# Neighbour maximum on TensorE: the key products of a step stand between the ranks and the second pick

## The chip, the cores and the metric

The kernel runs on one core of a Trainium2 chip. The metric is device time in microseconds (us) of one launch, with every input in device memory; the figure given for a kernel is the median of its runs.
## The reference

```python
def reference(x, adj, W, a):             # x (4096,128) f32, adj (4096,4096) int32, 0 or 1
    # layer 0: maximum over the neighbours, feature by feature
    h = jnp.maximum(_layernorm(x), 0.0)
    masked = jnp.where((adj != 0)[:, :, None], h[None, :, :], neg)
    x = x + jnp.max(masked, axis=1)       # in chunks of rows; 0 where a row has no neighbour
    # layer 1: graph attention
    h = jnp.maximum(_layernorm(x), 0.0)
    h = h @ W
    e = (h @ a[:128])[:, None] + (h @ a[128:])[None, :]    # a is (256, 1), one column
    e = jnp.where(e > 0, e, 0.2 * e)
    attention = jax.nn.softmax(jnp.where(adj > 0, e, -9e15), axis=1)
    return x + elu(attention @ h)
```

A row of `adj` has some 17 neighbours among 4096 columns. The change lies in layer 0, the neighbour maximum.

## The kernel before

Layer 0 goes over `adj` in 8 tiles of 512 rows (`TILES`), and over the columns of a tile in 16 pairs of 128-column chunks (`STEPS`): 128 steps g (`PAIRS`). Chunks of 128 columns hold few neighbours of a row, mostly none, one or two. A step picks the first and the second of them exactly by matmuls and raises a running maximum with them; what is left over (a third neighbour, and one that a shared second pick can't take) is left to a search by keys and to gathers from a table in device memory.

TensorE does these parts for a step, all in the function `_(pe)` of the tensor block:

- turns (`flip`, L581 to L594): 8 transposes of `adj` from `stage` into `flip_ps`, for step g + 5. They wait for the load, and for ScalarE's copy of the turned block before (`edge_ready`).
- ranks (`rank`, L596 to L606): 2 matmuls of 512 columns into `order_ps`, for step g + 3; in some steps (`shared`) a third, the nudge (L605). They wait until ScalarE has read `order_ps` of the step before (`depth_ready`).
- first and second pick (`pick`, L608 to L627): 4 matmuls of 512 columns each, with the high and the low half of h as weights, into `pick_ps[0]` and `pick_ps[1]`. Each waits until VectorE has taken the maximum of the same buffer in the step before (`raised`).
- key products (`digest(n, half)`, L629 to L641): 8 matmuls of 128 columns into `key_ps`. A group n covers two steps' `rest` masks and is done in two halves: half 0 in the even step g = 2n + 2, half 1 in the odd step 2n + 3. Half 0 waits for the masks and for `keyed`, n: ScalarE must have copied the keys of group n - 1 out of `key_ps`. For odd n it begins with one matmul of 512 columns, the word (L635). `flip_ps` and `key_ps` are the two halves of `late_ps`, one bank each.

ScalarE does in step g, in this order: `edges(g + 4)` (L393, copy of the turned block, waits for `flipped`), in even steps `key(g // 2 - 2)` (L423, copy of the keys, waits for `digested`), `select(g + 3)` (L404 `first` and L405 `depth`, waits for `ordered`, the ranks), and in even steps `later` (L413, masks).

VectorE does in step g: `take(g, 0)` (L882, the maximum with the first pick), then in some steps `rests` (L870) or `seconds` (L864), `take(g, 1)` (with the second pick; half as wide where `shared`), and after that, in some steps, a subset table entry (L857, steps 0 to 10), `fold` (L886, once in 16 steps), the `search` of keys (L890, once in four steps) and `halve_two` (L898 to L904, three of eight steps).

SyncE loads `stage` (L277, 1 MB for two steps, four stages, waits for `flipped`) and stores the turned edges for layer 1 (L284). GpSimd issues the gathers (L376), paced by `raised`. Each engine runs its list strictly in the order in which it is written out; the semaphores order the engines among each other.

The order on TensorE is written by hand, in the loop at L739: first pick of g, ranks of g + 3, second pick of g, turns of g + 5, key products. Layer 1 (L762 on) begins with the last key products and then mixes, for 256 blocks, weights that VectorE makes (L1072).

Of the kernel before, what the change touches and what calls it, by code (L numbers as in the profile page):

```python
# [86 lines left out]
def layers(nc, adj, x_rows, w, a, edge_units, subset_max, out_rows, w_sb, a12, w_in, hs, x1_in, h_hi, h_lo, ident_h, ident32, order_w, bit_w, word,  # L87
# [4 lines left out]
    with ctx:  # L92
# [73 lines left out]
        def rest_done(eng, m):  # L166
            if m % 2 == 0:
                eng.wait_ge(rest_even, m // 2 + 1)
            else:
                eng.wait_ge(rest_odd, 2 * (m // 2 + 1))  # L170
# [4 lines left out]
        def shared(g):  # L175
            return g % 8 in (2, 4, 6) or g < len(CHAINS)
# [10 lines left out]
        spare = lambda i: keys[:, 1, i, :].rearrange("p (g d) -> p g d", d=D) if i < ROWS else left[:, (i - ROWS) * GROUPS:(i - ROWS + 1) * GROUPS, :]  # L187
        saves = lambda i: 16 * (len(range(i, len(CHAINS), SPARES)) + (2 if i == 3 else 0))
        slot_of = {m: i % SPARES for i, (m, _, _) in enumerate(CHAINS)}
        many_of = lambda m: one_of(SINGLES[m]) if m in SINGLES else spare(slot_of[m])  # L190

# [80 lines left out]
        with nc.Block() as block:  # L272
# [307 lines left out]
            def _(pe):  # L580
                def flip(g):  # L581
                    n, s = g // KEEP, g % KEEP
                    if s == 0:
                        pe.wait_ge(landed[n % STAGES], 16 * (n // STAGES + 1))
                    if g == 0:
                        pe.wait_ge(consts_made, 1)
                    if g >= 1:
                        pe.wait_ge(edge_ready, g)
                    for c in range(PAIR):
                        for r in range(ROWS):  # L590
                            low = stage[:, n % STAGES, r, :].bitcast(F16).rearrange("p (j t) -> p j t", t=2)[:, :, 0]
                            last = nc.tensor.transpose(flip_ps[:, c * TI + r * P:c * TI + (r + 1) * P],  # L592
                                                       low[:, (s * PAIR + c) * P:(s * PAIR + c + 1) * P], ident_h[:, :])
                    last.then_inc(flipped, 1)  # L594

                def rank(g):  # L596
                    pe.wait_ge(edge_ready, g + 1)
                    if g >= 1:
                        pe.wait_ge(depth_ready, g)
                    for c in range(PAIR):  # L600
                        nudged = c == 1 and shared(g)
                        last = nc.tensor.matmul(order_ps[:, c * TI:(c + 1) * TI], order_w[:, :], edge_t[:, g % (KEPT * KEEP), c * TI:(c + 1) * TI],  # L602
                                                start=True, stop=not nudged)
                        if nudged:
                            last = nc.tensor.matmul(order_ps[:, TI:W], nudge_w[:, :], edge_t[:, g % (KEPT * KEEP), 0:TI], start=False, stop=True)  # L605
                    last.then_inc(ordered, 1)  # L606

                def pick(g, k):  # L608
                    p = g % STEPS
                    if k == 0:  # L610
                        pe.wait_ge(first_ready, g + 1)
                        if g < STEPS // 4:
                            pe.wait_ge(lo_first, 1)
                        elif g < STEPS:
                            pe.wait_ge(lo_ready, g * PAIR // EIGHTH - 1)
                    else:
                        pe.wait_ge(second_ready, g // 2 + 1)
                    if g >= 1:
                        pe.wait_ge(raised, 2 * (g - 1) + k + 1)
                    s = first[:, g % 4, :] if k == 0 else second[:, g % 4, :]  # L620
                    together = k == 1 and shared(g)
                    for c in range(PAIR):
                        to = 0 if together else c * TI
                        for part, half_h in enumerate((h_hi, h_lo)):
                            last = nc.tensor.matmul(pick_ps[k][:, to:to + TI], half_h[:, p * PAIR + c, :], s[:, c * TI:(c + 1) * TI],  # L625
                                                    start=part == 0 and not (together and c), stop=part == 1 and (c == 1 or not together))
                    last.then_inc(picked, 1)  # L627

                def digest(n, half):  # L629
                    if half == 0:  # L630
                        rest_done(pe, n)
                        if n >= 1:
                            pe.wait_ge(keyed, n)
                        if n % 2:
                            nc.tensor.matmul(key_ps[:, :], ones_h[:, :], word[:, :].rearrange("p (r w) -> p r w", r=1).broadcast_to((P, ROWS, P)), start=True, stop=False)  # L635
                    for r in range(half * ROWS // 2, (half + 1) * ROWS // 2):
                        for b in range(QUAD):
                            g, c = 2 * n + b // PAIR, b % PAIR
                            last = nc.tensor.matmul(key_ps[:, r * P:(r + 1) * P], rest[:, g % RESTS, c * TI + r * P:c * TI + (r + 1) * P],  # L639
                                                    bit_w[:, b, :], start=n % 2 == 0 and r == 0 and b == 0, stop=r == ROWS - 1 and b == QUAD - 1)  # L640
                    last.then_inc(digested, 1)  # L641

                def rows(g):
                    if g == 0:
                        pe.wait_ge(depth_ready, PAIRS)
                        pe.wait_ge(folded, 2)
                    elif g == 2:
                        pe.wait_ge(folded, 4)
                        pe.wait_ge(raised, 2 * PAIRS - 1)
                    elif g == 4:  # L650
                        pe.wait_ge(col_took, 4)
                    elif g == 5:
                        pe.wait_ge(limited, 3)
                    elif g == 6:
                        pe.wait_ge(col_took, 5)
                    elif g == LAST:
                        pe.wait_ge(folded, TILES)
                        pe.wait_ge(joined, LAST)
                    for c in range(ROWS):
                        last = nc.tensor.transpose(row_ps(g)[:, c * P:(c + 1) * P], best[:, (g * ROWS + c) * P:(g * ROWS + c + 1) * P], ident32[:, :])  # L660
                    last.then_inc(rows_put, 1)

                def columns(g):
                    if g == 0:
                        pe.wait_ge(small_took, 3)
                    elif g == 1:
                        pe.wait_ge(col_took, 1)
                    elif g in (2, 3):
                        pe.wait_ge(wh_made, ROWS)
                    elif g in (4, 5):  # L670
                        pe.wait_ge(joined, 6)
                    else:
                        pe.wait_ge(col_took, g)
                    pe.wait_ge(h_made, (g + 1) * ROWS)
                    for c in range(ROWS):
                        last = nc.tensor.transpose(col_ps(g)[:, c * P:(c + 1) * P], h[:, g * ROWS + c, :], ident32[:, :])
                    last.then_inc(col_put, 1)
# [61 lines left out]
                for g in range(PAIRS):  # L739
                    if g:  # L740
                        pick(g, 0)
                    if g + 3 < PAIRS:
                        rank(g + 3)
                    if g == PAIRS - 4:
                        pe.wait_ge(edge_ready, PAIRS)
                        pe.wait_ge(w_in, 48)
                        nc.tensor.transpose(wt_ps, w_sb[:, 0:D], ident32[:, :]).then_inc(small_put, 1)
                    if g == PAIRS - 3:
                        pe.wait_ge(small_took, 1)
                        pe.wait_ge(wide_made, 2)  # L750
                        nc.tensor.matmul(wa_ps, w_t[:, :], a_wide[:, :], start=True, stop=True).then_inc(small_put, 1)
                        rows(0)
                        rows(1)
                    pick(g, 1)
                    if g + AHEAD < PAIRS:
                        flip(g + AHEAD)
                    if g >= 2:
                        digest(g // 2 - 1, g % 2)
                columns(0)
                rows(2)  # L760
                rows(3)
# [549 lines left out]
```

## Time and profile before

| What | Value |
|---|---|
| median of 3 runs | 725.0 us (722.88 to 726.06) |
| the profiled execution | 728.94 us |
| its span, first to last instruction | 727.0 us |
| mean granted clock of TensorE | 0.990 |
| layer 0's steps | about 38 to 457 us of the span |
| mean DMA bandwidth | 227 GB/s |

All rows are of the profiled execution. Timelines give the start of an instruction and its recorded length; successive instructions of an engine are pipelined, so that recorded lengths overlap. The distance between two starts is what an instruction costs its engine when it does not wait. An idle time is given in brackets, with the engine and line that ended it.

### The profile page before, as it was taken

The numbers are of one execution on the slowest core, as the hardware profiler recorded it, in microseconds if no ns is written. First come the engines' busy times: TensorE is split into PE (matmuls) and PEld (weight loads), VectorE is DVE, ScalarE is ACT, GpSimd is POOL, SyncE is SP. The second block draws the span as 40 slices with busy tenths as digits, with TensorE's granted clock in tenths as the row PEclk, the third lists the DMA queues.
The fourth block names the chain that finished last, engine by engine and source line by source line (L and its number), as shares of the span: only waits on it lengthen the run. The fifth ranks groups of instructions, "written<-read, shape, count | busy, mean of one in ns | idle before, by whom it ended". The sixth has DMA issues, their size and how long they took to land.

```text
span 727.0 us, 14879 instructions
## 1 busy us (share of the span) xinstructions
PE 678.4 (93%) x5615; PEld 498.6 (69%) x5615; DVE 662.0 (91%) x1038; ACT 474.6 (65%) x692; POOL 265.4 (37%) x263
## 2 busy tenths in 40 slices
PE   1799999999999999999999997799989999999994
PEld 1355565656656556556555554798979999999994
DVE  8999799999999999999999999989987988888883
ACT  2898899999999999999999994644232301101100
POOL 0532046556555554556656563544410000000000
PEclk9999999999999999999999999999999999999997
DMA  9999988998889888888888646343423553435300
GB/s 300 302 354 387 389 284 286 325 363 287 270 272 288 292 276 286 258 284 291 287 275 273 210 142 240 94 145 128 143 89 105 189 198 131 174 132 181 124 16 18
DMA packets 64026, 165.19 MB, mean 227 GB/s; under 512 B 6929, under 2 KB 11665, under 8 KB 59857
## 3 DMA queue, kind: packets, MB, share of 16 engines
q1 hardware_dynamic: 53776, 138.75, 54.6%
q0 software_dynamic: 10176, 25.44, 13.3%
q8 instruction: 48, 0.79, 0.4%
q14 instruction: 26, 0.20, 0.1%
HBM read 119.60 MB, written 44.56 MB: 226 GB/s over the span
## 4 chain that ended last, share of the span: by engine, by line
PE 72%; DVE 13%; DMA 7%; issue 4%; ACT 3%; POOL 1%; DVEq 0%; SPq 0%; ACTq 0%; POOLq 0%
PE pick_ps L625 25%; PE pick_ps L726 21%; PE late_ps L592 6%; PE late_ps L639 6%; PE order_ps L602 6%; DVE acc L882 4%; PE late_ps L726 4%; DMA found<-subset_max,tops 4%; DMA edge_units<-edge_t 3%; DVE rest L1072 2%; PE order_ps L605 1%; POOL found L376 1%; ACT depth L405 1%; PE late_ps L635 1%; DVE acc L1001 1%
## 5 line engine op out<-in xcount | busy, mean ns | idle before, releaser
L376 POOL DMA_INDIRECT found<-subset_max,tops x224 | 238.0, 1062 | 222.0 <-DVE tops L890 102.9
L882 DVE TENSOR_TENSOR acc<-pick_ps,acc 128x1024 f32<-128x1024 f32 (+1 forms) x248 | 272.7, 1100 | 18.9 <-PE pick_ps L625 12.7
L726 PE MATMUL pick_ps<-keys,rest 128*128 128x129 f32 x1792 | 208.9, 277 | 7.2 <-DVE rest L1072 7.2
L726 PEld LDWEIGHTS pick_ps<-keys,rest 128*128 128x128 f32 x1792 | 204.9, 193 | 12.0 <-DVE rest L1072 9.5
L1072 DVE SCALAR_TENSOR_TENSOR rest<-depth,curves_sb,stage 128x512 f32<-128x512 f32 x256 | 183.1, 747 | 20.7 <-PE pick_ps L726 5.0
L404 ACT ACTIVATE first<-order_ps 128x1024 f16<-128x1024 f32 x128 | 131.3, 1025 | 16.3 <-PE order_ps L605 8.4
L405 ACT ACTIVATE depth<-order_ps 128x1024 f16<-128x1024 f32 x128 | 130.6, 1020 | 0.0
L592 PEld LDWEIGHTS late_ps<-ident_h,stage 128*128 128x128 f16 x1024 | 68.9, 100 | 49.9 <-DMA stage<-adj 13.1
L625 PE MATMUL pick_ps<-first,h_hi 128*128 128x512 f16 x256 | 97.5, 381 | 3.3 <-DVE acc L882 3.2
L625 PE MATMUL pick_ps<-second,h_hi 128*128 128x512 f16 x256 | 97.4, 381 | 3.1 <-DVE acc L882 3.0
L625 PE MATMUL pick_ps<-first,h_lo 128*128 128x512 f16 x256 | 97.5, 381 | 0.0
L625 PE MATMUL pick_ps<-second,h_lo 128*128 128x512 f16 x256 | 97.5, 381 | 0.0
L592 PE MATMUL late_ps<-ident_h,stage 128*128 128x128 f16 x1024 | 80.1, 222 | 17.4 <-DMA stage<-adj 13.1
L393 ACT ACTIVATE edge_t<-late_ps 128x512 int32<-128x512 int32 x128 | 77.1, 602 | 7.1 <-DMA edge_units<-edge_t 4.3
L602 PE MATMUL order_ps<-edge_t,order_w 128*128 128x512 f16 x256 | 77.5, 385 | 3.6 <-ACT depth L405 3.6
L639 PE MATMUL late_ps<-bit_w,rest 128*128 128x128 f16 x1024 | 78.3, 220 | 0.0
L518 ACT ACTIVATE keys<-pick_ps,acc 128x128 f32<-128x128 f32 x28 | 8.0, 368 | 100.0 <-DVE acc L1083 99.2
L639 PEld LDWEIGHTS late_ps<-bit_w,rest 128*128 128x128 f16 x1024 | 64.4, 98 | 5.4 <-issue 0.6
L413 ACT ACTIVATE rest<-depth 128x1024 f16<-128x1024 f16 x64 | 67.8, 1060 | 0.0
L381 POOL DMA_DIRECT2D out<-keys x7 | 5.4, 770 | 158.4 <-DVE keys L1105 158.4
L625 PEld LDWEIGHTS pick_ps<-second,h_hi 128*128 128x128 f16 x256 | 25.0, 98 | 38.7 <-issue 10.6
L602 PEld LDWEIGHTS order_ps<-edge_t,order_w 128*128 128x128 f16 x256 | 24.5, 98 | 35.3 <-issue 8.1
(152 smaller groups left out, 600.1 us busy)
## 6 DMA issues: line engine op xcount, KB each, us to landing
stage<-adj SPq DMA_DIRECT2D x64, 1024.0 KB, 7.1
edge_units<-edge_t SPq DMA_DIRECT2D x64, 512.0 KB
stage<-edge_units SPq DMA_DIRECT2D x32, 1024.0 KB, 4.8
subset_max<-keys POOLq DMA_DIRECT2D x9, 512.0 KB, 10.9
found<-subset_max,tops POOLq DMA_INDIRECT x224
best<-x SPq DMA_DIRECT2D x4, 512.0 KB, 6.1
subset_max<-x POOLq DMA_DIRECT2D x4, 512.0 KB, 7.6
subset_max<-left POOLq DMA_DIRECT2D x4, 512.0 KB, 9.8
```

Source lines behind the costliest of these rows:

```text
L376: nc.gpsimd.indirect_dma_start(found[:, n % NG, s, :], None, subset_max, bass.IndirectOffsetOnAxis(tops[:, n, s:s + 1], 0)).then_inc(gathe ...
L393: nc.scalar.activation(edge_t[:, g % (KEPT * KEEP), :].bitcast(I32), flip_i[:, :], ACT.Copy, scale=ONE_BITS).then_inc(edge_ready, 1)
L404: nc.scalar.activation(first[:, g % 4, :], order_ps[:, :], ACT.Sigmoid, scale=-SHARP, bias=SHARP * (0.5 - MARK)).then_inc(first_ready, 1)
L405: nc.scalar.activation(depth[:, g % 4, :], order_ps[:, :], ACT.Abs, bias=MARK - MID).then_inc(depth_ready, 1)
L413: nc.scalar.activation(rest[:, to, :], depth[:, g % 4, :], ACT.Sigmoid, scale=-STEEPER, bias=STEEPER * LATE).then_inc(rest_odd, 1)
L592: last = nc.tensor.transpose(flip_ps[:, c * TI + r * P:c * TI + (r + 1) * P], low[:, (s * PAIR + c) * P:(s * PAIR + c + 1) * P], ident_h[: ...
L602: last = nc.tensor.matmul(order_ps[:, c * TI:(c + 1) * TI], order_w[:, :], edge_t[:, g % (KEPT * KEEP), c * TI:(c + 1) * TI], start=True, ...
L625: last = nc.tensor.matmul(pick_ps[k][:, to:to + TI], half_h[:, p * PAIR + c, :], s[:, c * TI:(c + 1) * TI], start=part == 0 and not (toget ...
L639: last = nc.tensor.matmul(key_ps[:, r * P:(r + 1) * P], rest[:, g % RESTS, c * TI + r * P:c * TI + (r + 1) * P], bit_w[:, b, :], start=n % ...
L726: last = nc.tensor.matmul(out_ps(q, b), weight[:, n % WEIGHTS, b * P:(b + 1) * P], wh[:, c, :], start=c == 0 and starts(q, b), stop=c == C ...
L882: V.tensor_tensor(acc[:, q % 2, 0:cols], pick_ps[k][:, 0:cols], acc[:, q % 2, 0:cols], ALU.max).then_inc(raised, 1)
L1072: V.scalar_tensor_tensor(out=weight[:, n % WEIGHTS, :], in0=limit[:, q % 4, :], scalar=slope[:, c:c + 1], in1=units[:, m % EDGES, k * TI:( ...
```

## The change

The call of `digest` moves from the end of the step's body to the place between the ranks (and what is inserted in two of the last steps) and the second pick. Which key products a step does, all waits inside `digest`, `pick` and `flip`, and all other engines' lists stay as they were.

```diff
@@ -751,11 +751,11 @@
                         nc.tensor.matmul(wa_ps, w_t[:, :], a_wide[:, :], start=True, stop=True).then_inc(small_put, 1)
                         rows(0)
                         rows(1)
+                    if g >= 2:
+                        digest(g // 2 - 1, g % 2)
                     pick(g, 1)
                     if g + AHEAD < PAIRS:
                         flip(g + AHEAD)
-                    if g >= 2:
-                        digest(g // 2 - 1, g % 2)
                 columns(0)
                 rows(2)
                 rows(3)
```

## Rows read from the trace of the kernel before

**Rows 1.** The page, busy us by engine (share of the span) and instructions.
```profile
PE 678.4 (93%) x5615; PEld 498.6 (69%) x5615; DVE 662.0 (91%) x1038; ACT 474.6 (65%) x692; POOL 265.4 (37%) x263
```

**Rows 2.** Windows: stretch, length, busy us of PE, PEld, DVE, ACT, POOL; clock, DMA share, GB/s.
```profile
260.00:340.00 80.00, 79.43 (x665) 47.70 (x662) 77.16 (x86) 77.02 (x101) 43.16 (x43) 1.00 0.87 277
```

**Rows 3.** Timeline of TensorE, an odd step's end and an even step: start, us, engine, operation.
```profile
301.29 0.38 PE L625 MATMUL pick_ps<-second,h_hi 128*128 128x512 f16 x1
...
302.60 0.61 PE L639 MATMUL late_ps<-bit_w,rest 128*128 128x128 f16 x8
303.05 0.38 PE L625 MATMUL pick_ps<-first,h_hi 128*128 128x512 f16 x1
...
303.91 0.59 PE L602 MATMUL order_ps<-edge_t,order_w 128*128 128x512 f16 x2
304.34 0.38 PE L625 MATMUL pick_ps<-second,h_hi 128*128 128x512 f16 x1
...
305.65 0.38 PE L635 MATMUL late_ps<-word,ones_h 128*128 128x512 f16 x1
```

**Rows 4.** The chain that ended last, by time: first and last of twelve like pieces.
```profile
131.69 0.88 PE pick_ps L625 x4
...
415.95 0.88 PE pick_ps L625 x4
```

**Rows 5.** Timeline of TensorE, the step of the cycle in which it waits for VectorE.
```profile
316.55 0.59 PE L602 MATMUL order_ps<-edge_t,order_w 128*128 128x512 f16 x2
317.33 0.38 PE L625 MATMUL pick_ps<-second,h_hi 128*128 128x512 f16 x1 [0.19 <-DVE acc L882]
```

**Rows 6.** Timeline of VectorE ahead of that wait.
```profile
305.85 0.68 DVE L882 TENSOR_TENSOR acc<-pick_ps,acc 128x512 f32<-128x512 f32 x1
306.45 0.94 DVE L898 TENSOR_TENSOR found<-found 128x768 f32<-128x768 f32 x1
307.38 1.22 DVE L882 TENSOR_TENSOR acc<-pick_ps,acc 128x1024 f32<-128x1024 f32 x1
...
312.78 1.22 DVE L890 MAX8 tops<-keys 128x8 int32<-128x1024 f32 x1
313.92 0.41 DVE L904 TENSOR_TENSOR left<-found 128x256 f32<-128x256 f32 x1
314.24 1.22 DVE L882 TENSOR_TENSOR acc<-pick_ps,acc 128x1024 f32<-128x1024 f32 x1
...
315.97 1.22 DVE L882 TENSOR_TENSOR acc<-pick_ps,acc 128x1024 f32<-128x1024 f32 x1
```

**Rows 7.** Timeline of ScalarE beside the steps of rows 3 and rows 5.
```profile
301.49 1.02 ACT L404 ACTIVATE first<-order_ps 128x1024 f16<-128x1024 f32 x1
...
303.32 0.60 ACT L393 ACTIVATE edge_t<-late_ps 128x512 int32<-128x512 int32 x1
303.80 0.62 ACT L423 ACTIVATE keys<-late_ps 128x512 f32<-128x512 f32 x1
...
306.37 1.06 ACT L413 ACTIVATE rest<-depth 128x1024 f16<-128x1024 f16 x1
...
316.43 0.62 ACT L423 ACTIVATE keys<-late_ps 128x512 f32<-128x512 f32 x1
```

**Rows 8.** Timelines of ScalarE and TensorE near 79 us, behind a DMA.
```profile
78.34 0.60 ACT L393 ACTIVATE edge_t<-late_ps 128x512 int32<-128x512 int32 x1 [2.04 <-DMA edge_units<-edge_t]
78.84 0.59 ACT L423 ACTIVATE keys<-late_ps 128x512 f32<-128x512 f32 x1
...
79.00 0.62 PE L592 MATMUL late_ps<-ident_h,stage 128*128 128x128 f16 x8 [1.10 <-ACT edge_t L393]
...
79.57 0.61 PE L639 MATMUL late_ps<-bit_w,rest 128*128 128x128 f16 x8
...
81.41 0.59 PE L602 MATMUL order_ps<-edge_t,order_w 128*128 128x512 f16 x2 [0.36 <-ACT depth L405]
```

**Rows 9.** Timeline of VectorE at the end of layer 0, step 125.
```profile
438.99 1.23 DVE L882 TENSOR_TENSOR acc<-pick_ps,acc 128x1024 f32<-128x1024 f32 x1 [0.81 <-PE pick_ps L625]
```

## The prediction

> **What bounds the kernel now.** I read the page's busy shares first [rows 1]: TensorE is busy 93% of the span and VectorE 91%, so the page alone names no bound. The table of windows for the middle of layer 0 [rows 2] shows three engines close together: of 80 us TensorE is busy 79.4, VectorE 77.2, ScalarE 77.0, at a clock of 1.00, the full level of 2.4 GHz. Two things can thus set a step's time: TensorE's own work, or a loop of waits through two engines. So I went to the timelines and took the distance from one start to the next as an operation's price (recorded durations overlap).
>
> TensorE, in step g [rows 3]: first pick 0.86 (303.05 to 303.91), ranks 0.43 (303.91 to 304.34), second pick and turns 1.31 (301.29 to 302.60), of which the second pick, as large as the first, is 0.86 and the turns 0.45, key products 0.45 (302.60 to 303.05). Together 3.05 us. A single 512-column matmul is a quarter of 0.86, 0.215: the nudge adds one in three of eight steps, the word matmul one in two of eight. A cycle of eight steps is 24.4 + 1.1 = 25.5 us of pure issue. The chain that ended last repeats the same pieces every 25.84 us, twelve times [rows 4], where the first and the last of the twelve stand, 284.26 us apart. The missing 0.35 us is one visible wait per cycle: ranks start at 316.55 and could be followed at 316.98, but the second pick starts at 317.33, released by VectorE [rows 5]. It waits for the maximum of the previous step's second pick, which VectorE starts only at 315.97, because a search (1.14) and a halving (0.32) stood ahead of it in VectorE's order [rows 6]. So layer 0 is bound by TensorE's issue, plus 0.35 us in one step of eight.
>
> **The change, part by part.** Nothing is added or removed; the eight (or nine) key products of a step move ahead of second pick and turns, 1.31 us earlier in the step.
>
> (a) The wait on VectorE goes. In the step of 316.55 the key products, with their word, take 0.67 us, so the second pick is asked at 317.65 at the earliest, after 317.33. Gain 0.35 x 12 = 4.2 us. What is late next there? I laid VectorE's operations on the new order, (b) included, by [rows 6]: a maximum 1.13 and `seconds` or `rests` 0.60 (together 1.73, 314.24 to 315.97; the search, as wide as a maximum, is 1.14), a shared maximum 0.60, halvings 0.93, 0.60 (as wide as the shared maximum) and 0.32. Count from the start of a step g with g % 8 = 4: it and the next start at 0, 3.48, 6.53, 9.79 and 13.06, and a maximum starts 0.23 after its pick. VectorE ends its first maximum at 2.23, the shared one at 3.86, the halving at 4.79; in the next step maximum 5.93, `seconds` 6.53, maximum 7.67, halving 8.27; in the third maximum 9.41, shared maximum (from 9.57) 10.17, search 11.31, halving 11.63; in the fourth the maximum 12.77. The first pick at 13.06 needs that one, 0.15 us to spare with the 0.14 that (b) finds for a way between engines. Everywhere else there is more. So VectorE binds nowhere, by a small margin. The fold of every 16th step, 0.6 us, falls where VectorE has over 1 us of room.
>
> (b) A new wait comes, on ScalarE. The first half of the key products, in even steps, overwrites the PSUM region that ScalarE's key copy (L423) reads, and waits for `keyed`. ScalarE does, in an even step: edge copy, key copy, the two outputs of select, perhaps later. In the step of 303.05 the key copy starts at 303.80 and lasts 0.62, so it ends at 304.42 [rows 7]. Now the products are asked at 305.65, and it is long done. In the new order they are asked when the ranks end, at 304.34 [rows 3]: 0.08 us before the copy has ended. To that comes the way from ScalarE to TensorE. Two places near 79 us show it [rows 8]: the edge copy ends at 78.94 and the turns start at 79.00 (0.06); the key copy ends at 79.43 and key products that waited for it start at 79.57 (0.14). The second is the same pair of operations, so I take 0.14. The wait is 0.08 + 0.14 = 0.22 us. The step of the VectorE wait gives the same: copy 316.43 + 0.62 + 0.14 = 317.19 against 316.98, 0.21 [rows 5, 7]. The Trainium skill, page Perfetto Trace Analysis, section Per-instruction lifecycle, says that a semaphore reaches other engines after the recorded end of a ScalarE instruction; with that delay at nothing the wait would be 0.08 us a time and 4.3 us in all; the trace agrees with the page.
>
> Does this wait recur, or does ScalarE catch up once? I followed the loop from the odd step's ranks. They end at 301.29; first starts at 301.49 (0.20 later), select takes 1.83 to 303.32, the edge copy 0.48, the key copy 0.62, the way 0.14: 3.27 us from ranks to the moment the next even products may start [rows 3, 7]. TensorE's own path between the same two points is, in the new order, products, second pick, turns, first pick, ranks: 0.45 + 0.86 + 0.45 + 0.86 + 0.43 = 3.05. Both start at the same event, so the 0.22 returns in every pair of steps; in the old order the path had 1.31 more and hid it. The loop then goes on behind the wait through second pick, turns, first pick and ranks, and TensorE does not get the time back. ScalarE's own work of a pair (two selects of 1.83, two edge copies, key copy, `later` of 1.06 at most, each from [rows 7]) is at most 6.3 us, in truth less, as recorded durations overlap, against 6.3 or more for the pair, so it gives nothing back either. Could the edge copy be late, since its turns now end the previous step? They end 1.76 us after the ranks, plus 0.20 for the way 1.96, while ScalarE is free at 2.03: covered, by 0.07.
>
> The even steps 16 to 122 are 54. At 0.215 each: 11.6 us.
>
> (c) Steps before 16. Here stores of edges hold ScalarE up (2.04 us idle for a DMA) [rows 8], so a small wait ahead of such a place costs nothing. But at the last of them, near 78 us, second pick and turns used to come before the key products or right at the edge copy; now the products wait until 79.57 and both follow (0.86 + 0.45). The odd step's ranks had waited for ScalarE until 81.41, and ended at 82.05; in the new order they end at 79.57 + 0.45 + 1.31 + 0.86 + 0.65 = 82.84. Cost 0.8 us. For the two earlier places I take nothing, since the next store sets the time again. Bounds: 0 and 3 x 0.8 = 2.4.
>
> (d) The end of the stage. At step 124 the wait falls where TensorE next waits for ScalarE anyway. In step 125 the products stand before a second pick for which VectorE is idle 0.81 us [rows 9], and VectorE then runs the layer's end: +0.45. In steps 126 and 127 VectorE is far behind TensorE: nothing. Bounds 0 and 0.9 (twice 0.45).
>
> (e) Queues. Turns end 0.67 us or so later in a step, and with them the loads of `stage` that SyncE issues; a load has four stages, seven steps, ahead of its use. The stores wait for edge copies, which move with the step. GpSimd's gathers are paced by `raised`, which shifts by as little. Nothing. Layer 1 has the same order and moves as a block.
>
> Sum: 11.6 - 4.2 + 0.8 + 0.45 = 8.65 us. Against the profiled execution, span 727.0 gives 735.6 and its own 728.94 gives 737.6. The median of three runs, 725.0, lies 3.9 under that execution; on it I predict 733.6 us, 1.2% slower.
>
> **The rivals.**
> *The key copy is in time* (chance 0.12). If ScalarE's copy ran ahead by 0.22 us, from edges ready earlier or ranks that no longer start late, only (a) is left, with (c) and (d): -4.2 + 1.25 = -3.0, 722.0 us. It ends not slower. The place is the wait on `keyed` in even steps, its price 0.215 x 54; it decides at a copy that ends 0.22 earlier. For it: the miss is small beside a copy of 0.62. Against: both paths start at the same ranks [rows 3, 7], in all four even steps of the cycle.
> *The VectorE wait stays too* (0.15). If the 0.15 us of margin in (a) isn't there, TensorE waits for ScalarE in each even step and once per cycle for VectorE. At most the 4.2 of (a) come back: 737.8 us. For it: VectorE at 77.2 of 80 [rows 2]. Against: the longer cycle, about 26.3, gives VectorE 0.5 us more room.
> *The wait is longer than its two terms* (0.08). If the turns, now last in a step, make the edge copy late, say by 0.1 more than the 0.07 of cover, all 54 pairs get 0.1 longer: 5.4 us, 739.0 us.
> *The clock falls* (0.03). In the stretches with waits of 0.35 us the granted clock was 1.00 [rows 2, 5], the 2.4 GHz level. If the many short waits lowered it to 1.2 GHz in a tenth of layer 0's 350 us, issue there would take twice as long, 35 us: 769 us. The Trainium skill, page TensorE: Matmul & The Clock Gate, section A second HAM failure mode, tells of a kernel whose frequent micro-idles made the clock swing; by that rule this rival would be likely; the trace speaks against it as far as it goes.
>
> **How the numbers follow.** Forecast 0.62, the rivals 0.12, 0.15, 0.08 and 0.03. The forecast's own range: the wait between 0.14 (way 0.06) and 0.28 gives -4.1 and +3.5; (c) and (d) give -1.25 and +2.05: 728.3 to 739.2. The range of 8 in 10 takes in the third and part of the second case down to 727 and up to 740. A measurement tells 0.5%, about 3.6 us, from no change. Slower by more: the forecast nearly whole and three rivals, 0.83; within: most of the first rival and the low edge of the forecast, 0.13; faster by more: 0.04, a copy in time with (c) and (d) at nothing, 720.8.
>
> **What would show it.** In the timeline after: key products following the ranks with an idle of 0.2 us in even steps, released by ScalarE L423, and no idle before the products of odd steps; second picks without the wait on VectorE; a cycle of about 26.3 us in place of 25.84. (b) is wrong if the even products follow the ranks without idle; (a) if second picks still wait for VectorE; (c) if ranks near 82 us don't shift. I would be wrong altogether if the cycle fell under 25.84.

## The result, and the profile after

| | before | after |
|---|---|---|
| median of 5 runs | 725.36 us (722.88 to 726.06) | 732.34 us (731.36 to 733.41) |
| the profiled execution | 728.94 us | 733.41 us |
| its span | 727.0 us | 731.6 us |

The ratio of after to before is 1.0094, with a 95% interval of 1.0064 to 1.0125: slower by 7.0 us. The forecast was 733.6 us and slower. A second job gave the changed kernel (4 runs) 732.06 us beside 725.72 us, ratio 1.0099 (1.0063 to 1.0135). All ratios leave out the few executions over 1.5% above the fastest of their kernel, which the medians keep (at most one of a kernel, but two of twelve in the second job with the key copy first).

The page of after, busy shares; it answers to [rows 1] and says as little:

```profile
PE 683.4 (93%) x5615; PEld 495.4 (68%) x5615; DVE 664.0 (91%) x1038; ACT 478.8 (65%) x692; POOL 269.2 (37%) x263
```

The windows of after (stretch, length, busy us of PE, PEld, DVE, ACT, POOL, then clock, DMA share, GB/s), beside [rows 2]: TensorE looks exactly as busy, VectorE and ScalarE each a little less. The clock is 1.00 here, and over 84 to 440 us as well, so the rival of the falling clock is out.

```profile
260.00:340.00 80.00, 79.42 (x645) 45.95 (x643) 76.20 (x84) 76.46 (x99) 43.72 (x43) 1.00 0.90 277
```

TensorE's timeline of after, an odd step and the start of the next even one (start, us, engine, operation), to be held against [rows 3]:

```profile
303.55 0.59 PE L602 MATMUL order_ps<-edge_t,order_w 128*128 128x512 f16 x2
303.98 0.38 PE L605 MATMUL order_ps<-edge_t,nudge_w 128*128 128x512 f16 x1
304.20 0.61 PE L639 MATMUL late_ps<-bit_w,rest 128*128 128x128 f16 x8
304.65 0.38 PE L625 MATMUL pick_ps<-second,h_hi 128*128 128x512 f16 x1
...
305.51 0.61 PE L592 MATMUL late_ps<-ident_h,stage 128*128 128x128 f16 x8
305.96 0.38 PE L625 MATMUL pick_ps<-first,h_hi 128*128 128x512 f16 x1
...
306.82 0.59 PE L602 MATMUL order_ps<-edge_t,order_w 128*128 128x512 f16 x2
307.46 0.38 PE L635 MATMUL late_ps<-word,ones_h 128*128 128x512 f16 x1
```

In the odd step nothing waits: 303.98 + 0.215 = 304.20, the key products' start. In the even step the ranks take 0.43, to 307.25, and the products (their word) start at 307.46: a wait of 0.21 us. ScalarE's timeline names the cause, as [rows 7] foretold it:

```profile
304.40 1.02 ACT L404 ACTIVATE first<-order_ps 128x1024 f16<-128x1024 f32 x1
305.32 1.02 ACT L405 ACTIVATE depth<-order_ps 128x1024 f16<-128x1024 f32 x1
306.22 0.60 ACT L393 ACTIVATE edge_t<-late_ps 128x512 int32<-128x512 int32 x1
306.70 0.62 ACT L423 ACTIVATE keys<-late_ps 128x512 f32<-128x512 f32 x1
```

The odd ranks end at 304.20, `first` starts 0.20 later, the key copy ends at 307.32, and 0.14 later the products start. From ranks to products it is 3.26 us (predicted 3.27), against 3.05 of TensorE's own work. Two words that stand eight steps apart give the cycle:

```profile
307.46 0.38 PE L635 MATMUL late_ps<-word,ones_h 128*128 128x512 f16 x1
...
333.79 0.38 PE L635 MATMUL late_ps<-word,ones_h 128*128 128x512 f16 x1
```

26.33 us, where [rows 4] had 25.84. The wait on VectorE of [rows 5] is gone. The summary of waits (who waited, for whom: us in total, times, longest us) of before has it, 180 to 340 us:

```profile
PE pick_ps L625 <- DVE acc L882: 1.1, 6, 0.2
```

After has no such row between 180 and 420 us. Nor has it a row of matmuls for the new wait. It lists for TensorE only weight loads, put down to "issue", 180 to 340 us:

```profile
PEld late_ps L635 <- issue: 6.2, 12, 0.5
PEld late_ps L639 <- issue: 6.2, 12, 0.5
```

These two rows do point at the place. Before has none for L635 and L639 in this stretch, and their 24 times are one for each of its even steps. But they name no releaser, and 0.5 us is not what the wait costs.

The recorded length of the ranks, 0.59, covers most of a wait of 0.21 that begins 0.43 after their start. Only 0.05 is left as idle time, some twelve times in 80 us. That comes to the 0.58 us that TensorE is idle now, as the three recorded waits of 0.19 on VectorE made the 0.57 before: two different losses leave the same busy share. 54 waits of 0.21 are 11 us, and what each costs only the distance between starts shows.

### The profile page after: what moved, and what is told of

Read it like the earlier page. It is cut to its first block, busy times and chain, and to the rows that moved or that the text cites. A ratio compares the mean times of both kernels' runs of the same rounds, so it can differ in the third digit from the quotient of the medians.

```text
span 731.6 us, 14879 instructions
## 1 busy us (share of the span) xinstructions
PE 683.4 (93%) x5615; PEld 495.4 (68%) x5615; DVE 664.0 (91%) x1038; ACT 478.8 (65%) x692; POOL 269.2 (37%) x263
## 4 chain that ended last, share of the span: by engine, by line
PE 78%; DVE 8%; DMA 7%; ACT 3%; issue 2%; POOL 1%; SPq 0%; DVEq 0%; ACTq 0%; POOLq 0%
PE pick_ps L625 27%; PE pick_ps L726 21%; PE late_ps L639 8%; PE late_ps L592 7%; PE order_ps L602 7%; PE late_ps L726 4%; DMA found<-subset_max,tops 4%; DMA edge_units<-edge_t 2%; DVE rest L1072 2%; PE order_ps L605 1%; PE late_ps L635 1%; POOL found L376 1%; ACT depth L405 1%; DVE acc L1001 1%; DMA best<-x 1%
## 5 line engine op out<-in xcount | busy, mean ns | idle before, releaser
L376 POOL DMA_INDIRECT found<-subset_max,tops x224 | 241.0, 1076 | 223.7 <-DVE tops L890 108.0
L639 PEld LDWEIGHTS late_ps<-bit_w,rest 128*128 128x128 f16 x1024 | 66.1, 98 | 36.0 <-issue 17.3
L639 PE MATMUL late_ps<-bit_w,rest 128*128 128x128 f16 x1024 | 78.2, 219 | 3.0 <-ACT keys L423 1.6
L864 DVE TENSOR_SCALAR second<-depth 128x2048 f16<-128x2048 f16 x64 | 45.1, 705 | 0.0
```

The costliest lines, as they stand in the source:

```text
L376: nc.gpsimd.indirect_dma_start(found[:, n % NG, s, :], None, subset_max, bass.IndirectOffsetOnAxis(tops[:, n, s:s + 1], 0)).then_inc(gathe ...
```

## The experiments

The theory (K): the whole cost is the wait of the even key products for ScalarE's key copy, which recurs since both paths start at the odd ranks. The rival (T): the cost is that second pick or turns come later in the step. "Beside it" means runs of the kernel before on the same chip in the same job.

**The key copy first.** In ScalarE's list, even steps:

```diff
+                    if g % 2 == 0 and g >= 4:
+                        key(g // 2 - 2)
                     if g + AHEAD - 1 < PAIRS:
                         edges(g + AHEAD - 1)
-                    if g % 2 == 0 and g >= 4:
-                        key(g // 2 - 2)
```

> The changed kernel, with ScalarE's key copy ahead of the edge copy in even steps, nothing else. Theory K (the 0.22 us wait of the even key products on the key copy is the whole cost): the copy ends 0.48 us earlier, before the ranks end, so the wait goes; a cycle of eight steps is TensorE's issue, 25.5 us, the waits on VectorE stay away, and the time is below before by about 4: 721 to 723 us, some 10 under the changed kernel. Rival T (the cost is that second pick or turns come later in the step): nothing is gained, 731 to 733 us, cycle 26.3.

Measured: 725.13 us, beside it 727.20; ratio 0.9979 (0.9946 to 1.0011). In a second job, on the same chip, 722.99 beside 725.24; ratio 0.9960 (0.9931 to 0.9990). The cost is gone with nothing changed on TensorE, so T falls. The gain over before is 2 us, not the 4 of the expectation, and the first interval still holds 1: that there is a gain at all is shown by the cycle in both traces, more than by the times. TensorE's timeline of the first run:

```profile
302.39 0.59 PE L602 MATMUL order_ps<-edge_t,order_w 128*128 128x512 f16 x2
302.82 0.38 PE L635 MATMUL late_ps<-word,ones_h 128*128 128x512 f16 x1
...
313.72 0.61 PE L592 MATMUL late_ps<-ident_h,stage 128*128 128x128 f16 x8
314.24 0.38 PE L625 MATMUL pick_ps<-first,h_hi 128*128 128x512 f16 x1
```

The word follows the ranks at once (302.82 less 302.39 is 0.43). The first pick at 314.24 comes 0.08 later than 0.445 of turns allow; it is the step g % 8 = 0, the tight place that part (a) had worked out, at the end of VectorE's search step. The maximum that it needs stands there:

```profile
312.87 1.22 DVE L882 TENSOR_TENSOR acc<-pick_ps,acc 128x1024 f32<-128x1024 f32 x1
```

312.87 + 1.22 is 314.09, and 0.14 later the pick could start. The cycle is 25.57 instead of 25.48, and its gain on before 0.27 us, not 0.35. Near 150 us ScalarE waits for a store, 1.39 us in this trace and 2.73 in the second run's; the cycle around it is longer by 0.9 and 2.2 us:

```profile
149.50 0.60 ACT L393 ACTIVATE edge_t<-late_ps 128x512 int32<-128x512 int32 x1 [1.39 <-DMA edge_units<-edge_t]
```

The trace of after has no such wait there, the one of its repeat has one of 0.76, with a cycle 0.9 longer; what decides it was not tried.

**Turns before the key products, even steps.**

```diff
+                    if g % 2 == 0 and g + AHEAD < PAIRS:
+                        flip(g + AHEAD)
                     if g >= 2:
                         digest(g // 2 - 1, g % 2)
                     pick(g, 1)
-                    if g + AHEAD < PAIRS:
+                    if g % 2 and g + AHEAD < PAIRS:
                         flip(g + AHEAD)
```

> The changed kernel, with the turns of even steps between the ranks and the key products (order there: first pick, ranks, turns, key products, second pick); odd steps as changed, ScalarE's list untouched. Theory K: the even products are asked 0.45 us later than in the changed kernel, 0.23 after the copy is done, so the wait goes as in the run with the key copy first: cycle 25.5, 721 to 723 us, if the turns themselves don't wait for the edge copy (they are asked 0.36 us after its end). Rival T: the second pick of even steps is later still, so at least 732 us.

Measured: 730.66 us, beside it 727.20; ratio 1.0041 (1.0011 to 1.0071). Theory K missed the time. TensorE's timeline:

```profile
309.37 0.59 PE L602 MATMUL order_ps<-edge_t,order_w 128*128 128x512 f16 x2
309.81 0.61 PE L592 MATMUL late_ps<-ident_h,stage 128*128 128x128 f16 x8
310.25 0.61 PE L639 MATMUL late_ps<-bit_w,rest 128*128 128x128 f16 x8
310.70 0.38 PE L625 MATMUL pick_ps<-second,h_hi 128*128 128x512 f16 x1
...
311.96 0.38 PE L625 MATMUL pick_ps<-first,h_hi 128*128 128x512 f16 x1 [0.24 <-DVE acc L884]
```

What K says of the key copy holds: ranks, turns and products stand 0.44 apart, no wait. But the next first pick, asked at 311.56, waits until 311.96 for VectorE, and another 0.13 us is lost one step on. It needs the maximum with the first pick of the step before:

```profile
310.60 1.22 DVE L884 TENSOR_TENSOR acc<-pick_ps,acc 128x1024 f32<-128x1024 f32 x1
```

310.60 + 1.22 + 0.14 is 311.96. VectorE runs without a gap up to this maximum from 305.66 on, where it took the late second pick of an even step, 2.61 us after that step's ranks had started; with the key copy first it is 2.16 us. So VectorE stands 0.45 us later against TensorE, and the room at this place (0.05 us with the key copy first) was less than that. The cycle is 26.05 us. My expectation had checked the key copy and the edge copy, and not VectorE. The rival's "at least 732" is over the measured time too, but its mechanism, a second pick that is too late, is real once it stands behind the turns and the key products.

**One half at a time.** Only the key products of even steps moved, or only those of odd steps:

```diff
-                    if g >= 2:
+                    if g >= 2 and (g % 2 == 0):
                         digest(g // 2 - 1, g % 2)
...
+                    if g >= 2 and not (g % 2 == 0):
+                        digest(g // 2 - 1, g % 2)
```

> Only the key products of even steps are moved, those of odd steps stay behind the turns. Theory K: the path on TensorE from the odd ranks to the even ones is as long, so the even products still wait 0.22 us, the wait on VectorE in one step of eight is still hidden: cycle 26.3, 731 to 733 us, as the changed kernel. Rival T: half of the cost, about 728.5 us.

> Only the key products of odd steps are moved. Theory K: no products wait for the key copy; the wait on VectorE, which lies in an even step, stays at about 0.35 us in a cycle: cycle 25.84, 724.5 to 726.5 us, as before the change. Rival T: half of the cost, about 728.5 us.

Measured: even only 734.13 us, ratio 1.0089 (1.0051 to 1.0127); odd only 728.75 us, ratio 1.0016 (0.9981 to 1.0050); beside both 727.20. Even only, from its timeline:

```profile
303.34 0.59 PE L602 MATMUL order_ps<-edge_t,order_w 128*128 128x512 f16 x2
303.99 0.61 PE L639 MATMUL late_ps<-bit_w,rest 128*128 128x128 f16 x8
```

It waits 0.22 us (303.34 + 0.43 = 303.77) and has the cycle of 26.33. Odd only keeps the wait on VectorE and the cycle of 25.84:

```profile
317.37 0.59 PE L602 MATMUL order_ps<-edge_t,order_w 128*128 128x512 f16 x2
318.17 0.38 PE L625 MATMUL pick_ps<-second,h_hi 128*128 128x512 f16 x1 [0.20 <-DVE acc L884]
```

By the cycles theory K met both: the wait on the key copy appears, and the wait on VectorE goes, where the products of even steps are moved, and neither happens with the odd ones. By the times it met neither range: 734.13 is 1.1 over it, 728.75 is 2.3 over it and lands on the rival's figure of 728.5. But both ranges were set from a before of 725, and here before took 727.20. Against that, half of the cost would be a ratio near 1.005; the odd steps alone gave 1.0016, with 1.0050 at the edge of its interval, and the even ones 1.0089, the whole cost. What decides against "half each" is the pair of cycles, 26.33 and 25.84. One small piece of the cost does lie in an odd step, the end of the layer; see (d) below.

**The key copy later, in both orders.** Ahead of 52 of the key copies ScalarE does two copies of one column into a tile that nothing reads:

```diff
+                    if 8 <= n < 60:
+                        for k in range(2):
+                            nc.scalar.activation(pad[:, 2 * n + k:2 * n + k + 1], eps[:, :], ACT.Copy)
                     nc.scalar.activation(keys[:, q % 2, :, g * P:(g + 1) * P], key_ps[:, :]...
```

> The changed kernel, and ScalarE does two one-column copies right ahead of 52 of the key copies, for steps 20 to 122 (some 0.15 us each, by the small copies in the trace). Theory K: the key copy is on the loop, so each us that it comes later is paid in full: +0.3 us a pair, 52 pairs, +12 to +17 us over the changed kernel, 745 to 750 us. Rival T (turns or second pick being late is the cost): less than 4 us.

> The same two copies in the kernel before the change. Theory K: the key products come 1.31 us later in the step and hide them; what is left is that ScalarE's next select starts up to 0.1 us later in a pair: 0 to +5 us over before. If it costs as much as in the changed kernel, ScalarE's load and not the place of the key products is what counts, and theory K falls.

Measured: 742.09 us in the new order, 10.0 over the changed kernel in the same job (732.06; 4 runs each); 726.57 in the old order, ratio 1.0005 (0.9981 to 1.0029). ScalarE and TensorE in the new order:

```profile
305.82 0.31 ACT L426 ACTIVATE pad<-std_eps 128x1 f32<-128x1 f32 x2
...
306.00 0.60 ACT L427 ACTIVATE keys<-late_ps 128x512 f32<-128x512 f32 x1
...
306.75 0.61 PE L643 MATMUL late_ps<-bit_w,rest 128*128 128x128 f16 x8 [0.22 <-ACT keys L427]
```

The two copies shift the key copy by 0.18 us, not 0.3, so the expectation was too high; 52 x 0.18 = 9.4 us. The medians gave 10.0, the traces of this run and of after 9.2 between steps 16 and 124. The cycle is 27.02, 0.69 over 26.33, 0.17 a pair. Here the wait is long enough for the profile to name it. In the old order the trace keeps its 25.84 us: the same 0.18 us costs nothing. This is the clearest of the runs: the key copy is on the loop in the new order, to the full, and off it in the old one.

**The changed kernel again, and the new order in the first steps alone.**

> The changed kernel once more, for the trace of a second execution and for a comparison on the same chip as the runs beside it. Both theories expect the cycle of 26.33 us again and 731 to 736 us, 6 to 8 over before. If the first 16 steps are 1.4 us shorter because of the change, as the first trace of it shows against before, they are so again; if that was the chance of a store's landing, the difference there is another, between -2 and +2 us.

> The new order in steps 2 to 15 only, the old one from step 16 on. If the new order itself shortens the waits for stores of edges in the early steps, the stretch from the first output of select of step 0 to that of step 16 is 1.2 to 1.4 us shorter than before's 55.15, and the rest of the trace is before's (cycle 25.84): 1 to 1.5 us under before. If part (c) of the prediction was right, it is 0.8 us longer; if it is the chance of a landing, neither.

Measured: again 732.06 us, ratio 1.0099; the new order in steps 2 to 15 alone 725.14 beside 725.24, ratio 0.9998 (0.9966 to 1.0029). From the `first` that ScalarE makes in step 0 to the one of step 16 the traces give, in us:

| kernel | step 0 to 16 |
|---|---|
| before; with the slow key copy, old order | 55.15; 55.07 |
| after; again; with the slow key copy | 53.72; 53.95; 54.28 |
| new order in steps 2 to 15 alone | 54.61 |
| key copy first, its two runs | 54.53; 54.74 |
| the same with the old end, its two runs | 53.98; 55.37 |
| turns first in even steps | 52.95 |
| even steps only; odd steps only | 56.17; 55.78 |

The three traces of the new order agree on 0.9 to 1.4 us less, and the summary of waits between 40 and 100 us shows where: ScalarE's waits for stores are 1.5 us in after, and were 4.3 us in three before.

```profile
ACT edge_t L393 <- DMA edge_units<-edge_t: 1.5, 1, 1.5
```

But the run that was to isolate it gave 0.5 us, below what its time can tell, though its trace too has one wait for a store in place of three. The two halves went the other way. And the four traces with the key copy first have one and the same order in these steps and range from 53.98 to 55.37, a spread of 1.4 us, as large as the effect. So the +0.8 us of the prediction came in no trace of the changed kernel, and whether the order shortens this stretch or chance does stays open. That turns which end later let SyncE issue a load later, with less of it ahead of the next store, would fit; it was only argued.

**The version that remains.** Key copy first, and the key products of the last three steps in their old place:

```diff
-                    if g >= 2:
+                    if 2 <= g < PAIRS - 3:
                         digest(g // 2 - 1, g % 2)
...
+                    if g >= PAIRS - 3:
+                        digest(g // 2 - 1, g % 2)
```

> The changed kernel with the key copy first, and the key products of the last three steps where they were before the change. From the trace of the run with the key copy first: its cycle of 25.56 us stays, and the end of layer 0 loses the 0.44 us by which the second pick of step 125 had come later: 0.4 us under the run with the key copy first, ratio to before 0.994 to 0.999.

> The changed kernel with the key copy first, again, beside the next one on one chip: 0.2 to 0.5% under before; cycle 25.56 us.

> The same with the key products of the last three steps in their old place, again: by the traces 0.4 us under the run beside it; if the first pair of runs (722.3 and 725.1 us, on two chips) showed a real difference, 2 to 3 us under it.

Measured: 722.30 beside 725.72, ratio 0.9947 (0.9925 to 0.9969), and again 722.38 beside 725.24, ratio 0.9963 (0.9931 to 0.9995). Both intervals lie under 1, on two chips: this version beats the kernel before by about 3 us, and the changed kernel by some 10 (732.06 in the first of the two jobs). Against the key copy first alone, on one chip, 722.38 and 722.99 can't be told apart. The traces can: from `first` of step 124 to the last maximum of the layer it keeps before's distance, while the key copy first alone takes 0.43 us longer.

## Why the prediction was right, point by point

Forecast 733.6, measured 732.34; +8.65 us forecast, +7.0 by the medians, +4.6 between the two profiled spans. The main term was right in mechanism and size. That the whole came within 1.3 us is luck in part: term (c) was off by 2.2 us in the traces, and what lies outside the changed steps differs by 1.7 us between two executions.

| Term | predicted | between the two traces |
|---|---|---|
| (b) less (a), steps 16 to 124 | 11.6 - 4.2 = +7.4 | +7.3 |
| (c) steps before 16 | +0.8 | -1.4 |
| (d) end of layer 0 | +0.45 | +0.44 |
| before step 0, nothing changed there | 0 | -0.5 |
| the last gathers in layer 1 and what follows | 0 | -1.2 |

The steps' times are those of the `first` outputs: after stands 1.96 us ahead of before at step 16 and 5.34 behind at step 124. The repeat of after gives +8.1 in place of +7.3, of which 0.9 is the wait for a store near 150 us.

(b) was right in place, size and recurrence: the 0.08 us by which the copy was late, the 0.14 of the way as [rows 8] gave it, and the loop from odd ranks to even products, 3.26 for 3.27. The 49 even steps between 100 and 425 us wait 0.21 or 0.22 us each, the odd ones not at all. The runs show it from three sides: taken away (key copy first), lengthened one for one (slow key copy), split by halves (even only, odd only).

(a) was right: no second pick waits for VectorE, and the 0.15 us of margin held. How narrow it is showed when the key wait was taken away: then 0.08 us of waiting appears at that place.

(c) failed. The step at fault is the assumption that the stores land when they did before. I kept the wait of [rows 8] where it was (ScalarE idle 2.04 us near 78 us) and let the products run behind it; in after there is no such wait there, and the key copy runs from 76.17, with the products at 76.94. Why the store landed otherwise stays open:

```profile
76.17 0.62 ACT L423 ACTIVATE keys<-late_ps 128x512 f32<-128x512 f32 x1
...
76.94 0.61 PE L639 MATMUL late_ps<-bit_w,rest 128*128 128x128 f16 x8
```

The measured -1.4 lies outside the bounds 0 and 2.4; where a landing decides, the bounds need room below nothing.

(d) was right. VectorE's maximum of step 125, [rows 9], now waits 0.84 us and sits 5.78 us behind before's, 0.44 more than step 124:

```profile
444.77 1.23 DVE L882 TENSOR_TENSOR acc<-pick_ps,acc 128x1024 f32<-128x1024 f32 x1 [0.84 <-PE pick_ps L625]
```

The halves put it on the key products of step 125: from `first` of step 124 to the layer's last maximum it is 18.57 us before and with the even steps alone, 19.01 in after and with the odd steps alone.

(e) and "layer 1 moves as a block" were right within what the chain of the last gathers allows. From the last search to the last merge (L990) before takes 31.56 us, after 30.53, the repeat of after 28.84, odd only 31.46: serial gathers whose landings differ from one execution to the next, by more than the change's smaller terms.

Of the rivals, the key copy in time came out only where an experiment put it first, and then at -2 us, where its price said -3.0. The VectorE wait that stays was seen only in the run that moved the odd steps alone. The longer wait and the falling clock were not seen.

## What to carry to other kernels

Before a step of an in-order engine is moved ahead, look up for each of its waits when the releaser is done, and compare that with the new time of asking; 0.21 us are 11 us when the wait recurs 54 times. Whether it recurs follows from the two paths between the same two events: if the releaser's path starts at the mover's own earlier work, the wait is a loop and is paid each time. The gain of such a move can often be kept by moving the releaser instead: here one swap in ScalarE's list turned +7 us into about -2, and with the old end -3.

## What the runs showed of the hardware

Waits of 0.21 us on TensorE are covered, but for 0.05, by the recorded length of the matmuls before them. The busy time stayed at 79.4 of 80 us and the summary named no releaser; idle weight loads, one for each such wait, were the only sign. Waits of 0.35 us (before) and 0.38 us (slow key copy) did get a releaser, though with 0.19 and 0.22 us of idle time. A ScalarE operation on one column costs its engine 0.09 us here (two shift the next by 0.18), though each is recorded with 0.2 or so. The granted clock stayed at 1.00 from 84 to 440 us of after, with a wait of 0.21 us in each of its 54 pairs of steps.
